# Two stacked attention blocks on one core: first transfers and keyless test reordered, context loaded in 112 and 13 rows, another merged order of the steps

## Chip, core and metric

One core of a Trainium2 chip runs the whole kernel in one launch. The metric is the device time of a launch in microseconds, as the median of the runs. The kernel before has three runs: 367.54, 370.61 and 816.39 us, median 370.61. All work is in float32, apart from masks in bf16 and a split of some operands into a high and a low part (`fp32r`).

## What is computed

A batch of 8 sequences with 112 positions of 256 features, x, and a context of 375 positions each. Cut to what matters:

```python
# block 0: 16 heads of 16 features, causal, keys and values from the context
Q, K, V = relu(x @ Wq.T + bq), relu(ctx @ Wk.T + bk), relu(ctx @ Wv.T + bv)
scores = Q K^T / 4; masked where a key's feature sum is 0, and above the diagonal
out = softmax(scores) @ V * query_mask + x
x = layer_norm(out) * gamma + beta
# block 1
q, k, v = layernorm1(x) @ wqkv;  x1 = x + softmax(causal(q k^T / 16)) v @ wproj + b
q2 = layernorm2(x1) @ wq2;  k2, v2 = layernorm2(ctx) @ wkv2
x2 = x1 + softmax(q2 k2^T / 16) v2 @ wproj2 + b2
out = x2 + relu(layernorm3(x) @ w1 + b1) @ w2 + b3
```

With the causal mask a query of block 0 sees only the first 112 context positions. A query whose visible keys are all masked gets the mean over all 375 values. Only a sequence whose first context row sums to 0 can have one, so the kernel tests the 8 first rows for that and branches around a general path (the keyless test). With these inputs the branch is not taken.

## The kernel before, in words

The batch is worked in four groups g = 0 to 3 of two sequences b = 0, 1. Each engine (TensorE = PE, VectorE = DVE, ScalarE = ACT, GpSimd = POOL, SyncE = SP) walks the same list of 322 steps, `ORDER`, and does its own share of each step; semaphores tie the shares together. `ORDER` is merged from 15 streams by the string `MIX`, where each letter takes the next step of its stream. Each stream's own order is fixed; `MIX` alone says how they interleave.

- A and E (even and odd groups): `q0 k0 v0` (projections of block 0), `xT` (transpose), `q1 k1 v1`, `t1`, `proj`, `norm2`, `xqT`, `q2`.
- C, D, I, J (even/odd group, b = 0/1), self attention: `S` (scores on PE, maxima on DVE), `M` (maxima spread to rows), `X` (scores less the maximum on PE, exponentials on ACT, causal mask on POOL), `V` (sums with the values), `O` (ACT copies the sums, PE transposes, DVE divides), `dev`, `norm`, then the same for block 1's self attention.
- P, context: `stats`, `cnorm`, then for each b `cT` (transpose), `k2`, `v2`.
- B and F (b = 0/1), cross attention: four `cS` (scores, maxima), `cM`, three `cX` (exponentials) and `cV`, `cO`, `t2`, `y` (last projection and the store).
- H (`h`, feed forward in, two for each group), K (`f`, feed forward out, one for each sequence), W (`split` of the cross weights, `shift`), N (`keys`, `masks`, `late`), R (`rows`: a bias sum on DVE), L (`flag`, `general`: the keyless test and its branch).

An engine never passes a step of its own in `ORDER`. A step that writes to PSUM claims a bank or a pair of banks, the longest filled of three pairs (`ring`), and waits until that pair's reader is done. A pair is read by DVE for `S` and `cS` (two reductions for each step) and by ACT for `X` and `cX` (two exponentials).

The keyless test: DVE sums the 8 first rows and compares (L1190, L1192), PE adds up the eight results (`flag`, L573), DVE copies the count to `any_masked` (L1206), and then PE, DVE and SP each load it into a register and branch (`general`). In `keys` DVE sums the context rows (`ksum`, L960) and makes the masks `add_mask` (L970, L971), which `S` adds first (L597).

Transfers go out from two queues. SP issues inputs, weights and results in program order, waits included; ACT issues three small ones at the start, `first_keys`, `mask_u8` and `flat_c` (vectors of biases and the identity). Lines L413 `xk_t` (transposed inputs), L419 `x_nat`, L424 `keys_nat` (tile `xh`), L429 `c_nat` (context, 125 partitions of 6 KB: two sequences of three chunks), L437 `w_qk0`, L441 `w_v0`, L452 the cross weights, L473 `w_a`, L474 `rows_sb`, L476 `w_b`. Before all steps PE runs ten matmuls on zeros, `keep_busy(10)` (L802).

Of the kernel before, what the change touches and what calls it, by code (L numbers as in the profile page):

```python
# [102 lines left out]
def b_steps(g, b):  # L103
# [14 lines left out]

MIX = ("LAALNNCANDEECDCNPICWNCWDPJEWJICPDDICPJDNDIPIAJPIAAAJCJIHHJDERPCDECEDCJDCDPAIAAKAHIJNAAAPBPBEJABPJIFFIBJICPBFEFPBEBPBBBFN"
       "DENPFBFPBEFPFEBEDCPBFBFDNKFPCDFBFBCBDCHPBDEBCKBBDCFAPBAFBFPAFDACPNBCFDCPDCPJDCBIDBBNAFAFFFJIFAAJAEIFBJFPBKFBFBIFJIPHHBPJ"  # L120
       "BIJIPEKBEEFJHIBBBIJPIBJEFIFJIJBEPFEEFBKEFEFFBBBFBFFBHBFPBFFBFFFBBBFBFKBFFFBFFBFKFF")

# [83 lines left out]
def build(nc, xk_t_d, x_nat_d, keys_d, c_nat_d, c_t_d, c_first_d, mask_d, w_d, flat_d, mask_const_d, row_d, out_d):  # L206
    ctx = ExitStack()
    with ctx:
# [195 lines left out]
        def _(sp):  # L404
# [21 lines left out]
            def load_context(g):  # L426
                if g:
                    sp.wait_ge(*a_ct.done(g - 1))
                sp.dma_start(c_nat[:, :, :, :].rearrange("p b c u -> p (b c u)"), c_nat_d[g]).then_inc(c_loaded, 16)  # L429

# [4 lines left out]
            for part in range(2):  # L435
                load_x(0, part)
                sp.dma_start(w_qk0[:, part, :, :].rearrange("p c u -> p (c u)"), w_d["qk0"][:, part * C * U:(part + 1) * C * U]).then_inc((q0_loaded, k0_loaded)[part], 16)  # L437
            sp.wait_ge(xq_loaded[0], 16)
            load_keys(0)
# [6 lines left out]
            load_x(1, 1)  # L446
            sp.wait_ge(v0_loaded, 16)
            load_context(0)
            sp.wait_ge(xk_loaded[1], 16)
            load_keys(1)  # L450
            load_queries(1)
# [44 lines left out]
        def _(pe):  # L496
# [307 lines left out]
            pe.wait_ge(prep_dve, 1)  # L804
            keep_busy(10)
            run({"shift": shifts, "flag": flag, "general": general, "f": hidden_out, "masks": masks, "q0": project_q0, "k0": project_k0, "v0": project_v0, "S": self_scores, "M": self_max_rows, "X": self_shifted,
# [7 lines left out]
        def _(act):  # L814
# [109 lines left out]

            act.dma_start(first_keys, c_first_d).then_inc(first_loaded, 16)
            act.dma_start(mask_u8[:, :], mask_d).then_inc(mask_loaded, 16)
            act.dma_start(flat_c[:, :], flat_d).then_inc(flat_loaded, 16)
# [10 lines left out]
        def _(dve):  # L938
# [12 lines left out]
            def keys(g):  # L951
                s = v_mask
                if g == 0:
                    dve.wait_ge(pads_made, 1)
                dve.wait_ge(keys_loaded[g % 2], g // 2 * 16 + 16)
                if g > 1:
                    for b in range(G):
                        dve.wait_ge(*a_exp[b].done(g - 2))
                both = slice(slot(g, 0), slot(g, G))
                s.step(nc.vector.reduce_sum(ksum[:, both], keys_nat[g % 2][:, :, :], AX.X), g, 1)  # L960
                s.step(nc.vector.tensor_copy(pad1[:, both], pad1_all[:, g * G:(g + 1) * G]), g, 2)
                after(s, g)
                s.step(nc.vector.tensor_scalar(keep0b[:, both], ksum[:, both], 0.0, None, ALU.not_equal), g, 3)
                s.step(nc.vector.tensor_scalar(pad0[:, both], ksum[:, both], 0.0, BIG, ALU.is_equal, ALU.mult), g, 4)
                s.step(nc.vector.tensor_scalar(keep1b[:, both], pad1[:, both], 0.0, None, ALU.is_equal), g, 5)
                after(s, g)
                for b in range(G):
                    if g == 0 and b == 0:
                        dve.wait_ge(mask_const_loaded, 16)
                    s.step(nc.vector.tensor_scalar(add_mask[:, 0, slot(g, b), :], causal[:, :], pad0[:, slot(g, b):slot(g, b) + 1], None, ALU.min), g, 6 + 2 * b)  # L970
                    s.step(nc.vector.tensor_scalar(add_mask[:, 1, slot(g, b), :], causal[:, :], pad1[:, slot(g, b):slot(g, b) + 1], None, ALU.min), g, 7 + 2 * b)  # L971
# [164 lines left out]
            def context_statistics(g):  # L1136
                s, n = v_ctx, G * NCH
                dve.wait_ge(c_loaded, g * 16 + 16)
                for i in range(n):
# [47 lines left out]
            for i in range(2):  # L1187
                nc.vector.memset(acc[i][:, :, :], 0.0).then_inc(prep_dve, 1)
            dve.wait_ge(first_loaded, 16)
            nc.vector.reduce_sum(first_sum[:, :], first_keys, AX.X).then_inc(flag_steps, 1)  # L1190
            dve.wait_ge(flag_steps, 1)
            nc.vector.tensor_scalar(first_masked[:, :], first_sum[:, :], 0.0, None, ALU.is_equal).then_inc(flag_steps, 1)  # L1192
            dve.wait_ge(mask_loaded, 16)
            nc.vector.tensor_scalar(pad1_all[:, :], mask_u8[:, :], BIG, None, ALU.mult).then_inc(pads_made, 1)
            dve.wait_ge(prep_act, 2)
            for e in range(2):
                nc.vector.tensor_scalar(bq0_eo[:, :, e], vec[:, VEC["bq0"]:VEC["bq0"] + C], eo_scale[:, 0, e:e + 1], None, ALU.mult).then_inc(prep_dve, 1)

# [5 lines left out]
            def general():  # L1204
                dve.wait_ge(flag_counted, 1)
                nc.vector.tensor_copy(any_masked[:, :], gen_s[:, 0:1]).then_inc(flag_made, 1)  # L1206
                dve.wait_ge(flag_made, 1)
# [102 lines left out]
```

## Time and profile before

| what | value |
|---|---|
| runs | 367.54, 370.61, 816.39 us |
| the profiled execution, its own time | 368.39 us |
| its span, first to last instruction | 366.6 us |
| outside the span | 1.8 us |
| granted TensorE clock over the span | 0.999 |
| PE busy | 346.7 us (95%) |
| DVE busy | 224.4 us (61%) |
| ACT busy | 170.6 us (47%) |
| POOL busy | 52.3 us (14%) |

All times in rows below are microseconds from the start of the span unless marked ns. A busy PE is not a PE at its peak, since a matmul record can contain time in which the next one could not yet start.

### The profile page before, as it was taken

What the parts mean: (1) busy time and instruction counts of PE and PEld (TensorE: products, weight loads), DVE (VectorE), ACT (ScalarE), POOL (GpSimd) and SP (SyncE); (2) the same over time, 40 slices, a digit from 0 to 9 for tenths busy, and PEclk for the clock granted to TensorE, in tenths of its full rate; (3) what the DMA queues carried; (4) which work ended last, traced back from release to release, by engine and by line L of the source; (5) the groups of instructions that cost most, each with busy time, mean ns of one, the idle gap of its engine ahead of it and who ended that gap; (6) DMA issues with size and microseconds to landing.
All of it is one profiled execution on the core that took longest, in us unless ns stands there. A gap on an engine that the chain in (4) does not pass through costs nothing.

```text
span 366.6 us, 9692 instructions
## 1 busy us (share of the span) xinstructions
PE 346.7 (95%) x4144; PEld 262.0 (71%) x4144; DVE 224.4 (61%) x563; ACT 170.6 (47%) x299; POOL 52.3 (14%) x67
## 2 busy tenths in 40 slices
PE   7978899999999999999999999999999999999996
PEld 4656688877965677876876786766987768675674
DVE  3879898426768746566945758556944464264412
ACT  2266652560674155674454062763453644614350
POOL 2024331040032010122100041130100031000000
PEclk9999999999999999999999999999999999999999
DMA  6759302000000002000000200000000000000000
GB/s 194 221 172 355 112 16 98 0 4 0 27 0 2 2 6 82 27 14 15 3 2 6 80 2 14 4 2 13 1 4 0 2 2 2 15 2 13 4 2 25
DMA packets 5300, 14.12 MB, mean 39 GB/s; under 512 B 689, under 2 KB 2982, under 8 KB 5002
## 3 DMA queue, kind: packets, MB, share of 16 engines
q1 hardware_dynamic: 4970, 13.42, 11.2%
q8 instruction: 33, 0.54, 0.6%
q10 hardware_dynamic: 288, 0.09, 0.1%
q14 instruction: 9, 0.07, 0.1%
HBM read 12.59 MB, written 0.92 MB: 37 GB/s over the span
## 4 chain that ended last, share of the span: by engine, by line
PE 76%; DVE 13%; DMA 5%; ACT 2%; issue 2%; SPq 1%; POOL 0%; DVEq 0%
PE ring L502 35%; PE ring L744 8%; PE acc L648 8%; PE ring L758 5%; PE ring L623 5%; DVE negmax L1032 4%; PE ring L603 3%; PE ring L597 3%; DMA xh<-in_keys 3%; PE ring L635 2%; DVE negmax L1011 2%; PE ring L667 2%; DMA w_qk<-in_w_qk 2%; PE ring L615 1%; PE ring L709 1%
## 5 line engine op out<-in xcount | busy, mean ns | idle before, releaser
L1032 DVE TENSOR_REDUCE negmax<-ring 112x2 f32<-112x750 f32 x64 | 57.0, 936 | 23.3 <-PE ring L744 22.6
L857 ACT ACTIVATE exps<-ring 125x896 f32<-125x896 f32 x48 | 41.4, 915 | 39.5 <-PE ring L758 39.2
L1247 POOL TENSOR_SCALAR_AFFINE_SELECT exps<-exps 112x896 f32<-112x896 f32 x32 | 30.9, 989 | 118.2 <-ACT exps L857 118.2
L1011 DVE TENSOR_REDUCE negmax<-ring 112x8 f32<-112x896 f32 x32 | 33.4, 1085 | 22.2 <-PE ring L603 22.1
L744 PE MATMUL ring<-k,q 32*112 32x376 f32 x256 | 38.4, 518 | 1.3 <-ACT exps L857 0.5
L648 PE MATMUL acc<-exps,v 125*17 125x112 f32 (+1 forms) x1280 | 38.7, 261 | 0.2
L648 PEld LDWEIGHTS acc<-exps,v 125*17 125x17 f32 (+1 forms) x1280 | 28.1, 97 | 12.7 <-issue 10.3
L857 ACT ACTIVATE exps<-ring,pad 112x896 f32<-112x896 f32 x32 | 30.5, 1003 | 11.3 <-PE ring L635 11.2
L502 PE MATMUL ring<-w_b,h 128*112 128x256 f32 x128 | 29.3, 382 | 0.0
L502 PEld LDWEIGHTS ring<-w_b,h 128*112 128x112 f32 x128 | 22.1, 177 | 5.8 <-issue 1.1
L502 PE MATMUL ring<-n,w_b 128*128 128x224 f32 x128 | 25.7, 357 | 0.2
L894 ACT ACTIVATE h<-ring,flat_c 128x224 f32<-128x224 f32 x32 | 11.7, 448 | 29.9 <-PE ring L502 29.9
L744 PEld LDWEIGHTS ring<-k,q 32*112 32x112 f32 x256 | 14.2, 169 | 15.2 <-issue 8.6
L502 PEld LDWEIGHTS ring<-n,w_b 128*128 128x128 f32 x128 | 23.7, 190 | 1.6 <-issue 1.4
L623 PE MATMUL ring<-maxrows,sel 32*125 32x224 f32 (+1 forms) x320 | 22.6, 318 | 1.2 <-DVE negmax L1011 0.5
L758 PE MATMUL ring<-q,k 32*125 32x224 f32 x384 | 23.1, 349 | 0.0
L623 PEld LDWEIGHTS ring<-maxrows,sel 32*125 32x125 f32 (+1 forms) x320 | 14.2, 175 | 10.7 <-issue 6.9
L502 PE MATMUL ring<-n,w_a 128*128 128x224 f32 x96 | 20.7, 362 | 0.4 <-DVE negmax L1032 0.2
L597 PE MATMUL ring<-mask_c,add_mask 112*112 112x448 bf16 x64 | 16.6, 364 | 3.5 <-DVE add_mask L971 1.1
L502 PE MATMUL ring<-wkv,ct 128*125 128x256 f32 x144 | 19.2, 287 | 0.3 <-DVE negmax L1032 0.3
L1232 POOL TENSOR_TENSOR rstd<-var_e,half 112x1 f32<-112x1 f32 x16 | 9.2, 577 | 71.6 <-DVE var_e L1124 51.5
L502 PE MATMUL ring<-ct,wkv 128*128 128x376 f32 x96 | 18.4, 341 | 0.8 <-issue 0.7
(139 smaller groups left out, 544.9 us busy)
## 6 DMA issues: line engine op xcount, KB each, us to landing
c_nat<-in_ctx SPq DMA_DIRECT2D x4, 750.0 KB
w_b<-in_w_b SPq DMA_DIRECT2D x1, 2304.0 KB, 13.3
xk_t<-in_xk_t SPq DMA_DIRECT2D x8, 224.0 KB, 4.9
w_a<-in_w_a SPq DMA_DIRECT2D x1, 1280.0 KB, 7.0
xh<-in_keys SPq DMA_DIRECT2D x4, 224.0 KB, 4.3
x_nat<-in_x SPq DMA_DIRECT2D x4, 224.0 KB, 3.2
out<-x SPq DMA_DIRECT2D x8, 112.0 KB, 1.9
rows_sb<-in_row SPq DMA_DIRECT2D x1, 560.0 KB, 8.8
```

The source lines that it names most:

```text
L502: m = nc.tensor.matmul(dst, lhs, rhs, start=start and n == 0, stop=n == len(pairs) - 1, skip_group_check=True)
L597: nc.tensor.matmul(bank(r)[0:T, 0:4 * T], add_mask[:, l, slot(g, b), :], ident_b[:, :].unsqueeze(1).to_broadcast([T, 4, T]), start=True, s ...
L603: m = nc.tensor.matmul(bank(r)[0:T, j * T:(j + 1) * T], qf[g % 2][32 * r:32 * r + 32, c, b, e, :], kf[g % 2][32 * r:32 * r + 32, c, b, :], ...
L623: nc.tensor.matmul(bank(r)[0:k, 2 * c * T:2 * (c + 1) * T], sel[rows, c:c + 1].to_broadcast([32, k]), maxrows[i][rows, :], start=c == 0, s ...
L648: m = nc.tensor.matmul(acc[s][32 * p:32 * p + VW, 2 * c + m_, 0:T], vals(8 * c + 2 * r + e), exps[0:k, EXP_AT[job], rr, j * T:(j + 1) * T] ...
L744: m = nc.tensor.matmul(bank(r)[0:T, 0:SP], q2[g % 2][rows, c, b, e, :], k2[g % 2][rows, b, c, :], start=True, stop=True)
L758: m = nc.tensor.matmul(bank(r)[0:CH, 2 * c * T:2 * (c + 1) * T], k2[g % 2][rows, b, c, ch * CH:(ch + 1) * CH], q2[g % 2][rows, c, b, :, :] ...
L857: return nc.scalar.activation(exps[0:k, EXP_AT[job], :, :], o[0:k, :, 0:4 * T], ACT.Exp, bias=bias)
L894: a_h.step(nc.scalar.activation(h[g % 2][:, 4 * i0 + i, :, :].rearrange("p b t -> p (b t)"), o[:, i // 2, (i % 2) * G * T:(i % 2 + 1) * G ...
L1011: v_max[b].step(nc.vector.tensor_reduce(negmax[0][:, slot(g, b), 2 * m_:2 * m_ + 2, :], o[0:T, :, 0:4 * T].rearrange("p r (j t) -> p r j t ...
L1032: x_max[b].step(nc.vector.tensor_reduce(negmax[1][:, b, 2 * m_:2 * m_ + 2, i], o[0:T, :, 0:S], AX.X, ALU.max, negate=True), g, 2 * i + m_ + 1)
L1247: p_masked[b].step(nc.gpsimd.affine_select(e, e, [[0, 8], [1, T]], ALU.is_ge, 0.0, base=0, channel_multiplier=-1), g, k)
```

## The change

Five edits. (1) `MIX` is another string: the same 322 steps, otherwise interleaved. (2) SP's first transfers: `mask_u8` and `first_keys` move from ACT's queue to SP's, behind the `w_qk0` pieces, and take the place of a wait for `xq_loaded`; `load_keys(1)` goes ahead of `load_context(0)` and so ahead of the wait for `xk_loaded[1]`. (3) `load_context` issues 112 rows and 13 rows as two transfers, each adding 16 to `c_loaded`. (4) `keep_busy(8)` for `keep_busy(10)`. (5) The keyless test: DVE makes `bq0_eo` before the masks and first sums; the copy to `any_masked` moves from `general` into `keys(0)`, behind the key masks and ahead of `add_mask`; and `MIX` now starts q0, k0, flag, keys(0), masks(0), general, where it started flag, q0, k0, general, keys(0), masks(0).

Of the rest of the new order: steps 6 to 13 are the old ones with the two `M` swapped. In the stretch after, sequence b = 1 of group 0 goes ahead of b = 0, where b = 0 went first; `keys(1)`, `stats(0)` and `S(1,0,0)` keep places 15, 16, 17. `rows` is step 49 (was 60), `stats(1)` 68 (was 87), `v0(3)` 173 (was 217). `keys(2)` stands right behind `xqT(0)`; `h(1,0)` and two `M` steps stood between them. The last steps on PE were

```text
y(2,1) cS(3,1,0) cX(3,0,1) cS(3,1,1) cS(3,1,2) cS(3,1,3) cV(3,0,0) cX(3,0,2) cV(3,0,1) cM(3,1) cV(3,0,2) cX(3,1,0) f(3,0)
cO(3,0) cX(3,1,1) cV(3,1,0) cX(3,1,2) t2(3,0) cV(3,1,1) cV(3,1,2) y(3,0) cO(3,1) f(3,1) t2(3,1) y(3,1)
```

and are now

```text
y(2,1) cS(3,1,0) cX(3,0,0) f(3,0) cX(3,0,1) cS(3,1,1) cS(3,1,2) cS(3,1,3) cV(3,0,0) cX(3,0,2) cV(3,0,1) cM(3,1) cV(3,0,2) cX(3,1,0) f(3,1)
cO(3,0) cX(3,1,1) cV(3,1,0) cX(3,1,2) t2(3,0) cV(3,1,1) cV(3,1,2) cO(3,1) y(3,0) t2(3,1) y(3,1)
```

```diff
-MIX = ("LAALNNCANDEECDCNPICWNCWDPJEWJICPDDICPJDNDIPIAJPIAAAJCJIHHJDERPCDECEDCJDCDPAIAAKAHIJNAAAPBPBEJABPJIFFIBJICPBFEFPBEBPBBBFN"
-       "DENPFBFPBEFPFEBEDCPBFBFDNKFPCDFBFBCBDCHPBDEBCKBBDCFAPBAFBFPAFDACPNBCFDCPDCPJDCBIDBBNAFAFFFJIFAAJAEIFBJFPBKFBFBIFJIPHHBPJ"
-       "BIJIPEKBEEFJHIBBBIJPIBJEFIFJIJBEPFEEFBKEFEFFBBBFBFFBHBFPBFFBFFFBBBFBFKBFFFBFFBFKFF")
+MIX = ("AALNNLCANDEECDCDNPIWDNDWCPJEWJIDPCCJPDICJNCPJIAPAJRAAIPCIHDJIHEPECDECPEDCJDCDIAHJIPAAJKANIAABIBJBIJPABEFCAFPBNFBEBBFPBBFC"
+       "PFBFEPNDPBEFFBDECNFDFPBBFKFPBNFBDBCFDCPHEBDEBCPBCDBFAEFAJAFCADPBBDFCPDBCNPFCIDCBDPFFAJIFAJFIFABPAKFBPAKFBIBFBJBIJPHHBIPB"
+       "JIJKEPBEEFIHJBBBIJPIBJEFIFIBJFJBPFBEFEFEPEFEFFBBFBFKFBHBFFBKBFFFBBBFBFKBFFFBFFBFFF")
...
-                sp.dma_start(c_nat[:, :, :, :].rearrange("p b c u -> p (b c u)"), c_nat_d[g]).then_inc(c_loaded, 16)
+                for rows in (slice(0, 112), slice(112, CH)):
+                    sp.dma_start(c_nat[rows, :, :, :].rearrange("p b c u -> p (b c u)"), c_nat_d[g][rows, :]).then_inc(c_loaded, 16)
...
-            sp.wait_ge(xq_loaded[0], 16)
+            sp.dma_start(mask_u8[:, :], mask_d).then_inc(mask_loaded, 16)
+            sp.dma_start(first_keys, c_first_d).then_inc(first_loaded, 16)
             load_keys(0)
...
             sp.wait_ge(v0_loaded, 16)
+            load_keys(1)
             load_context(0)
             sp.wait_ge(xk_loaded[1], 16)
-            load_keys(1)
             load_queries(1)
...
-            keep_busy(10)
+            keep_busy(8)
...
-            act.dma_start(first_keys, c_first_d).then_inc(first_loaded, 16)
-            act.dma_start(mask_u8[:, :], mask_d).then_inc(mask_loaded, 16)
             act.dma_start(flat_c[:, :], flat_d).then_inc(flat_loaded, 16)
...
+                if g == 0:
+                    dve.wait_ge(flag_counted, 1)
+                    nc.vector.tensor_copy(any_masked[:, :], gen_s[:, 0:1]).then_inc(flag_made, 1)
+                    dve.wait_ge(mask_const_loaded, 16)
                 for b in range(G):
-                    if g == 0 and b == 0:
-                        dve.wait_ge(mask_const_loaded, 16)
...
-                dve.wait_ge(c_loaded, g * 16 + 16)
+                dve.wait_ge(c_loaded, g * 32 + 32)
...
+            dve.wait_ge(prep_act, 2)
+            for e in range(2):
+                nc.vector.tensor_scalar(bq0_eo[:, :, e], vec[:, VEC["bq0"]:VEC["bq0"] + C], eo_scale[:, 0, e:e + 1], None, ALU.mult).then_inc(prep_dve, 1)
+            dve.wait_ge(mask_loaded, 16)
+            nc.vector.tensor_scalar(pad1_all[:, :], mask_u8[:, :], BIG, None, ALU.mult).then_inc(pads_made, 1)
             dve.wait_ge(first_loaded, 16)
...
             def general():
-                dve.wait_ge(flag_counted, 1)
-                nc.vector.tensor_copy(any_masked[:, :], gen_s[:, 0:1]).then_inc(flag_made, 1)
                 dve.wait_ge(flag_made, 1)
```

## Rows read from the trace of the kernel before

**Rows 1.** The page, part 1: busy time of each engine over the span.

```profile
PE 346.7 (95%) x4144; PEld 262.0 (71%) x4144; DVE 224.4 (61%) x563; ACT 170.6 (47%) x299; POOL 52.3 (14%) x67
```

**Rows 2.** Windows by stage: length, busy time, PEclk, DMA share, GB/s.

```profile
0.00:10.00 10.00, 7.35 (x28) 4.18 (x28) 4.22 (x20) 3.26 (x7) 2.08 (x7) 1.00 0.66 197
10.00:50.00 40.00, 33.59 (x444) 25.91 (x444) 34.95 (x114) 21.38 (x39) 11.75 (x13) 1.00 0.58 193
50.00:330.00 280.00, 273.59 (x3236) 209.69 (x3236) 173.35 (x412) 132.76 (x234) 38.50 (x47) 1.00 0.04 14
330.00:366.60 36.60, 32.20 (x440) 22.26 (x438) 11.91 (x20) 13.23 (x21) 0.00 (x0) 0.99 0.04 11
```

**Rows 3.** Chain of waits, first 45 us: start, length, what it waited for.

```profile
2.21 5.92 DMA w_qk<-in_w_qk
...
8.97 3.67 DMA xk_t<-in_xk_t
12.65 9.85 DMA xh<-in_keys
```

**Rows 4.** Waits of DVE, 9 to 52 us: total, times, longest.

```profile
DVE ksum L960 <- DMA xh<-in_keys: 2.5, 2, 1.6
DVE negmax L1011 <- PE ring L603: 1.4, 1, 1.4
```

**Rows 5.** Timeline of SP's issues: start, length, line, operation.

```profile
9.64 0.28 SPq L429 DMA_DIRECT2D c_nat<-in_ctx  x1
...
52.67 0.32 SPq L429 DMA_DIRECT2D c_nat<-in_ctx  x1
```

**Rows 6.** Windows around large transfers, columns as in Rows 2.

```profile
24.40:30.20 5.80, 4.71 (x98) 3.42 (x96) 5.70 (x21) 2.30 (x4) 3.11 (x3) 1.00 1.01 341
...
53.00:62.00 9.00, 9.00 (x75) 7.81 (x74) 8.02 (x22) 2.13 (x4) 1.62 (x3) 1.00 0.34 114
```

**Rows 7.** Timeline of all engines, 8 to 14 us: start, length, [idle before].

```profile
8.16 1.78 PE L502 MATMUL ring<-xk_t,w_qk 128*128 128x224 f32 x8 [1.33 <-DMA w_qk<-in_w_qk]
8.27 0.15 DVE L1206 CAST any_masked<-acc 1x1 int32<-1x1 f32 x1
...
9.33 0.69 DVE L960 TENSOR_REDUCE ksum<-xh 112x2 f32<-112x512 f32 x1 [0.92 <-DMA xh<-in_keys]
...
11.07 0.94 PE L597 MATMUL ring<-mask_c,add_mask 112*112 112x448 bf16 x4 [0.25 <-DVE add_mask L970]
...
13.02 2.09 DVE L1011 TENSOR_REDUCE negmax<-ring 112x8 f32<-112x896 f32 x2 [1.42 <-PE ring L603]
```

**Rows 8.** Timeline, POOL at 24 us: mask of the first exponentials.

```profile
24.18 1.99 POOL L1247 TENSOR_SCALAR_AFFINE_SELECT exps<-exps 112x896 f32<-112x896 f32 x2 [21.50 <-ACT exps L857]
```

**Rows 9.** Line L802, keep_busy: ns min/median/max, first and last start.

```profile
L802 PE MATMUL ring<-acc_sb x10: 379/621/634, 1.3 to 4.6; 128*128 128x512 bf16 x10
```

**Rows 10.** Groups, cS on DVE and PE: busy, mean ns, idle before.

```profile
L1032 DVE TENSOR_REDUCE negmax<-ring 112x2 f32<-112x750 f32 x64 | 57.0, 936 | 23.3 <-PE ring L744 22.6
...
L744 PE MATMUL ring<-k,q 32*112 32x376 f32 x256 | 38.4, 518 | 1.3 <-ACT exps L857 0.5
```

**Rows 11.** Timeline of DVE at 96 us: the keys of group 2.

```profile
96.30 0.69 DVE L960 TENSOR_REDUCE ksum<-xh 112x2 f32<-112x512 f32 x1 [2.42 <-DMA xh<-in_keys]
```

**Rows 12.** Timeline of PE near the end: cS, cO after cV, f.

```profile
321.71 0.90 PE L744 MATMUL ring<-k,q 32*112 32x376 f32 x8
...
324.26 0.62 PE L667 MATMUL ring<-flat_c,acc_sb 128*112 128x128 f32 x4 [0.76 <-ACT acc_sb L875]
...
358.41 3.62 PE L502 MATMUL ring<-w_b,h 128*112 128x256 f32 x16
```

**Rows 13.** Chain of waits, 334 to 340 us.

```profile
334.79 0.95 DVE negmax L1032
...
336.97 0.93 ACT exps L857
...
338.87 0.95 DVE negmax L1032
```

More of the change, by code:

```diff
@@ L117 @@
            "R": [("rows",)], "L": [("flag",), ("general",)]}
-MIX = ("LAALNNCANDEECDCNPICWNCWDPJEWJICPDDICPJDNDIPIAJPIAAAJCJIHHJDERPCDECEDCJDCDPAIAAKAHIJNAAAPBPBEJABPJIFFIBJICPBFEFPBEBPBBBFN"
-       "DENPFBFPBEFPFEBEDCPBFBFDNKFPCDFBFBCBDCHPBDEBCKBBDCFAPBAFBFPAFDACPNBCFDCPDCPJDCBIDBBNAFAFFFJIFAAJAEIFBJFPBKFBFBIFJIPHHBPJ"
-       "BIJIPEKBEEFJHIBBBIJPIBJEFIFJIJBEPFEEFBKEFEFFBBBFBFFBHBFPBFFBFFFBBBFBFKBFFFBFFBFKFF")
+MIX = ("AALNNLCANDEEDCDNPIWDNDWCPJEWJIDPCCJPDICJNCPJIAPAJRAAIPCIHDJIHEPECDECPEDCJDCDIAHJIPAAJKANIAABIBJBIJPABEFCAFPBNFBEBBFPBBFC"
+       "PFBFEPNDPBEFFBDECNFDFPBBFKFPBNFBDBCFDCPHEBDEBCPBCDBFAEFAJAFCADPBBDFCPDBCNPFCIDCBDPFFAJIFAJFIFABPAKFBPAKFBIBFBJBIJPHHBIPB"
+       "JIJKEPBEEFIHJBBBIJPIBJEFIFIBJFJBPFBEFEFEPEFEFFBBFBFKFBHBFFBKBFFFBBBFBFKBFFFBFFFBFF")
 def merged():
@@ L1192, in _ @@
             nc.vector.tensor_scalar(first_masked[:, :], first_sum[:, :], 0.0, None, ALU.is_equal).then_inc(flag_steps, 1)
[L1193 to L1197, printed above, removed]
             def rows_summed():
```

## Prediction

> **What bounds the kernel now.** I read the page's engine line first, then windows by stage, then for each stage the chain of waits or the waits of the engine that the windows point at. Over the whole span PE is busy 346.7 of 366.6 us and nothing else is near that [rows 1]. So no reordering can win much: what it can win is PE's idle time, 19.9 us, and the waits that hide inside PE's busy records. The windows say where the idle time lies [rows 2]: 2.65 us before 10 us, 6.41 us from 10 to 50, 6.41 us in the 280 us of the middle, 4.4 us in the last 36.6. The reader is to see that the stage from 10 to 50 us is another kernel than the rest: DVE works 34.95 of 40 us there, and DVE, not PE, is the one that runs without a break. In the middle PE is at 98% and DVE at 62%.
>
> In that second stage DVE's waits have names [rows 4]: 1.4 us for the first scores, and 2.5 us in two waits for the context rows `xh` (L960), the longest 1.6. By subtraction the other is 0.9, the one at 9.33 us [rows 7]; so the 1.6 us belongs to the keys of group 1. The chain of waits shows why they are late [rows 3]: SP stands 3.67 us until `xk_t` of group 1 is in, issues the keys only at 12.65, and they need 9.85 us to land, at 22.5. What they queue behind is `c_nat`, issued at 9.64 [rows 5].
>
> **Context in two transfers.** The `c_nat` issued at 52.67 [rows 5] shows what that load is: 9 us at a DMA share of 0.34 and 114 GB/s, together 1.03 MB, which is the context and one load of queries (0.23 MB), while large weight transfers reach a share of 1.01 and 341 GB/s [rows 6]. So 125 partitions keep about a third of the 16 DMA engines busy and the keys behind them share those. The Trainium skill (DMA: Bandwidth & Descriptors, section on why a DMA increments its semaphore by 16) says that the number of engines is the largest up to 16 that divides the slowest dimension: 5 for 125, 16 for 112, 13 for 13. The trace's 0.34 agrees with 5 of 16. By my rows: 768 KB (750 KiB) at the 192 to 245 GB/s class of this stage (197 before 10 us, 193 after [rows 2]) is 3.9 us in place of about 9. Cost: one more issue on SP, 0.3 us [rows 5], four times, with nothing queued behind it on SP that is urgent. For groups 1 to 3 the gain is nil: no DVE wait on `c_nat` stands among the waits [rows 4], and the steps between `cT` and the next `stats` cover even 9 us. If that cover were gone in one group it would cost at most the present 9 us less the new 4, and the change makes that less likely, not more. In group 0 the split is what keeps `c_nat` from delaying `stats(0)`, queries and cross weights; it is worth its part of the next term.
>
> **Keys of group 1 ahead of the context.** They are issued at about 9.7 in place of 12.65, behind three loads of 224 KB that are in at 12.6 (8.97 + 3.67 [rows 3]); one more of that size at 197 GB/s takes 1.2 us, so they land at about 14, seven us before DVE asks (22.5 - 1.6 = 20.9). What is next late? The context follows to about 18, queries of group 1 (229 KB) to 19, cross weights (524 KB) to 22; their users come at 22.7 (`stats(0)`) and 23.2 or later (`split`). So DVE's 1.6 us go entirely: DVE does `keys(1)`, `stats(0)` and the maxima of `S(1,0,0)` 1.6 us earlier. PE does not collect it at once, since the first `V` waits for POOL's mask at 24.18 + 1.99 [rows 8], which hangs on ACT and not on the keys; but the stage is DVE's, and from its chain the gain reaches PE when PE becomes the bound at 50 us. **Term: -1.6 us**, bounds 0 (all swallowed by the POOL and ACT chain) and -2.5 (all of DVE's DMA waits).
>
> **Keyless test and first transfers.** Two things move against each other. DVE now enters `keys(0)` without the register load and branch that it made between 8.42 (end of L1206) and 9.33 [rows 7]; the key sums can start when the keys land. But `flag` on PE is now behind `k0`, whose weights land at 8.13 (2.21 + 5.92 [rows 3]) and which ends at 8.16 + 1.78 = 9.94. Two tiny matmuls and their signal take some 0.2 us, the copy 0.15, so the count is there at 10.3, and `add_mask` behind it at 10.4, about as now. Then PE has to load the count and branch before `S(0,0,0)`: the same operation took DVE at most 0.91 (8.42 to 9.33), so PE reaches S at 10.3 + 0.9 = 11.2, against 11.07 now [rows 7]. DVE's own branch falls into its 1.42 us wait for these scores, so it is covered; without that cover it would cost 0.9. SP keeps the place of its keys: two issues of 0.43 replace a wait that ended at the same time. `mask_u8` and `first_keys` land later (about 8), with 0.7 us of DVE work behind them, just before `keys(0)` starts; who waits behind them is `keys(0)`, which waits for its rows anyway. `flat_c` is issued a us earlier; its users run ahead of `k0`'s weights and win nothing. **Term: +0.2 us**, bounds -0.4 and +0.7.
>
> **keep_busy(8).** The two matmuls removed stood ahead of `q0`, and after `q0` PE waits 1.33 us for `k0`'s weights [rows 7]: hidden, 0. The ten of L802 take from 634 down to 379 ns, median 621 [rows 9]: most at the lower level (1.2 GHz), a few at 2.4 GHz. I take these to be the last ones, so the clock rises within the ten, and the 1.33 us of idle time after `q0` did not lower it, since `k0` took its 1.78 us at PEclk 1.00. The Trainium skill (TensorE: Matmul & The Clock Gate, Part 1) says that the clock rises only after PE has been busy for a while and falls after idleness; a shorter warm-up speaks against this edit. It is a rival below.
>
> **The last steps.** `f(3,0)`, 3.6 us [rows 12], now stands ahead of the run of four `cS`, and no `f` stands behind `cO(3,1)`. Gain: that run is bound by the readers of its banks; 0.95, 0.93 and 0.95 us of the chain there are DVE and ACT, not PE [rows 13]. With 3.6 us of other PE work in between, the first DVE piece goes for sure, the ACT piece perhaps, the last not, because three `cS` still follow each other: -0.95 to -1.9. Loss: `cO(3,1)` now stands right behind `cV(3,1,2)` and waits for ACT's copy, which the same pair cost 0.76 at 324.26 [rows 12]; `y(3,0)` still covers DVE's division behind it. Net between -1.1 and +0.8 (if the run of `cS` gains nothing); I take **-0.3**.
>
> **The middle order.** PE's visible idle time is 6.41 us, but `cS` hides more: 38.4 us over 32 steps is 1.20 us each [rows 10], where one that did not wait took 0.90 [rows 12]: 9.6 us. DVE needs 2 x 0.936 = 1.87 us for each, twice what PE needs, so each `cS` wants about 1 us of other PE work beside it. I counted in both orders the `S` and `cS` steps that directly follow another one: 7 before, 6 now. Elsewhere distances change both ways: `h` to its `f` and `q1` to `S` get tighter in one group each, `cO` to `t2` too, `X` to `V` looser. `keys(2)` right behind `xqT(0)` makes DVE wait up to 3.5 us in place of 2.42 [rows 11], with an `X` and two projections of 1.78 us each [rows 7] as cover. The context going in faster changes nothing here. **Term: -0.5 us**, bounds -4 and +5: half of the hidden waits either way.
>
> **Sum.** Against the profiled execution, 368.4 us (span 366.6 and 1.8 around it): -1.6 + 0.2 + 0 - 0.3 - 0.5 = -2.2, so **366.2 us**. The median of the runs before, 370.6, lies 2.2 above that execution and the fastest run 0.9 below it, and I forecast on the scale of the profiled one; a median that lies as high again would be 368.4.
>
> **Rivals.**
> *The gain is swallowed.* The 1.6 us are lost to POOL and ACT, whose first mask [rows 8] does not move, or to a new late load. For it: PE's `V` waits there. Against it: DVE, not PE, is busy without break. 366.2 + 1.6 = 367.8.
> *Slower: the cS of the new middle wait longer.* Place: `cS` behind `cS` or `S`, PE waiting for DVE's reductions. Price: half as much again as the 9.6 us hidden now, +4.8, hence 366.2 + 4.8 = 371.0. It decides from 2.2 us on, that is from a mean of 1.27 us for each `cS`. Against it: one fewer direct pair, and the same average load.
> *Faster: the new middle clears half of these waits.* 366.2 - 4.8 = 361.4.
> *The clock stays low.* With eight matmuls the rise comes only in or after `k0`. `k0` at half the rate adds 1.78 us on the path, 368.0, more if it lasts. Against: some of the ten are fast, and `q0` follows closely on the eighth.
>
> **How the numbers follow.** Chances: forecast 0.60 (own range 364.5 to 368.4), swallowed 0.14, slower middle 0.12, faster middle 0.11, clock 0.03. The range leaves out half of the two middle rivals' cases and takes in the higher median: 362.8 to 370.2. Two per cent, about what a measurement of this kernel can tell from no change, is 7.4 us of 370.6. Faster by more than that needs under 363.2: most of the faster middle, 0.09. Slower by more needs over 378: 0.02. Within: 0.89.
>
> **What the profile after should show.** SP issues the keys of group 1 before 10 us and they land before 15; DVE's wait for `xh` at 22.5 is gone, `stats(0)` starts near 22.7 and PE's idle time from 10 to 50 falls by 1 to 2 us. After `c_nat` of group 1 the DMA share is near 1 for some 3 us. `S(0,0,0)` starts at 11.0 to 11.5. PE stands about 0.8 us before `cO(3,1)`. Mean `cS` between 1.1 and 1.25 us. The prediction is wrong if `cS` leaves that band, if another transfer than the keys holds DVE before 30 us, or if the first matmuls after `q0` run at the lower clock.

## The result and the profile after

Six runs of the kernel after lie between 363.47 and 364.18 us, median **364.1**. Six of the kernel before, three of them new, have a median of 367.35. The ratio, which leaves out the run of 816.39 us, is 0.9903, interval 0.9877 to 0.9929: 1% faster, 3.3 us, inside the forecast's range and 2.1 us under its 366.2, and within the two per cent that it named as the likely class. The profiled execution took 364.14 us (span 362.4, which is 4.2 less than before, where the forecast had 2.2). The two numbers differ because the profiled execution of the kernel before, 368.39 us, lies 1.0 above the median of its runs, and that of the kernel after does not: some 0.9 of the 4.2 belongs to that one execution. In code lines of after, most lines of before are two higher: L744 is L746, L1011 is L1013.

The page's engine line and the windows by stage answer to [rows 1] and [rows 2].

```profile
PE 345.5 (95%) x4142; PEld 263.0 (73%) x4142; DVE 228.0 (63%) x563; ACT 170.9 (47%) x299; POOL 52.7 (15%) x67
```

```profile
0.00:10.00 10.00, 8.11 (x28) 5.22 (x28) 5.37 (x28) 3.95 (x9) 2.08 (x7) 1.00 0.76 185
10.00:50.00 40.00, 35.23 (x480) 26.86 (x480) 35.95 (x109) 21.95 (x40) 11.69 (x13) 1.00 0.59 195
50.00:330.00 280.00, 274.68 (x3244) 212.28 (x3244) 177.96 (x413) 132.84 (x235) 38.97 (x47) 1.00 0.05 15
330.00:362.40 32.40, 27.50 (x398) 18.67 (x392) 8.74 (x16) 12.19 (x17) 0.00 (x0) 0.99 0.03 9
```

PE's idle time fell from 19.9 to 16.9 us: 0.8 before 10 us, 1.6 from 10 to 50, 1.1 in the middle, while the end has 0.5 more. The other 1.2 us left PE's busy records, in which waits hide.

The start: the chain of waits of after (first group), its timeline (second), SP's issues (third) and DVE's waits from 9 to 52 us (fourth), beside [rows 3 to 5] and [rows 7].

```profile
1.26 3.60 PE ring L804 x8
4.86 2.66 PE ring L504 x8
7.63 1.82 ACT qf L829 x4
...
20.44 0.59 DVE ksum L960
...
22.21 1.98 DVE c_stats L1142 x6
```

```profile
4.65 4.37 PE L504 MATMUL ring<-xk_t,w_qk 128*128 128x224 f32 x16
...
10.46 0.94 PE L599 MATMUL ring<-mask_c,add_mask 112*112 112x448 bf16 x4 [0.98 <-ACT kf L822]
```

```profile
8.68 0.33 SPq L424 DMA_DIRECT2D xh<-in_keys  x1
9.05 0.88 SPq L430 DMA_DIRECT2D c_nat<-in_ctx  x2
```

```profile
DVE negmax L1013 <- PE ring L605: 2.0, 1, 2.0
DVE sd L1081 <- POOL sd_r L1232: 0.2, 1, 0.2
```

No DMA stands among DVE's waits from 9 to 52 us any more. The wait for `k0`'s weights, 1.33 us [rows 7], is gone as well: `q0` and `k0` are now one run of 16 matmuls, and what `S(0,0,0)` waits for is ACT's copy of `kf`. It starts at 10.46, 0.6 earlier than before, where I had 0.1 later.

The groups of `cS`, beside [rows 10]:

```profile
L1034 DVE TENSOR_REDUCE negmax<-ring 112x2 f32<-112x750 f32 x64 | 56.9, 935 | 19.3 <-PE ring L746 18.8
...
L746 PE MATMUL ring<-k,q 32*112 32x376 f32 x256 | 37.8, 518 | 1.3 <-DVE negmax L1034 0.5 <-ACT exps L859 0.4 <-ACT qf L829 0.3
```

1.18 us for each `cS` where it was 1.20. The end on PE, beside [rows 12], and the chain there, beside [rows 13]:

```profile
356.10 0.62 PE L669 MATMUL ring<-flat_c,acc_sb 128*112 128x128 f32 x4 [0.76 <-ACT acc_sb L877]
```

```profile
328.14 0.95 DVE negmax L1034
...
335.22 0.93 ACT exps L859
...
337.13 0.95 DVE negmax L1034
```

The forecast 0.76 is there, and all three pieces of DVE and ACT are still in the chain.

**Where the 4.2 us come from.** To compare two orders I took the start of each projection in a trace and subtracted the PE work of all steps ahead of it, at one fixed price for a step (0.9 us for a `cS`, 3.0 for an `h`, and so on from their undisturbed records). What is left is time that PE lost up to there; the mean over 24 us of work, less that of before, is the lead. It is good to some 0.4 us; a column mixes what happens within 12 us of work on either side of it. All of it is one execution against one, and that of before is 1.0 above its median. The last column is the difference of the spans.

```text
PE work done before (us)   10    50    110   170   230   290   span
after                      1.1   2.0   3.5   2.6   4.9   4.9   4.2
old order, edits 2 to 5    0.6   0.4   0.4   0.3   0.3   0.3   0.3
new order alone           -1.6  -1.3   0.2  -0.7   1.6   1.6   0.9
only keys(1) moved         0.3   0.8   0.8   0.8   0.8   0.9   0.8
after, keys(1) back        1.5   2.4   3.8   2.9   5.2   5.3   4.5
after, one context load    2.0   2.8   4.3   3.4   5.7   5.7   4.6
after, both of these       1.1   1.5   3.0   2.1   4.4   4.4   3.3
new to step 133, then old  1.7   2.6   4.1   3.9   3.9   3.9   3.9
old to step 133, then new  1.5   2.0   2.0  -2.1   0.2   0.3  -0.5
```

The first two columns can be read without a price, since up to `v1(0)` both orders often have the same kinds of step behind them. There the kernel after is ahead by 0.6 us at each step from `S(0,0,0)` to `k0(1)`, and by 1.6 at each of `v0(1)`, `k2(0,0)`, `q1(0)` and `v1(0)`. At `q0(1)` and at `v1(0)` the lead is 1.0 and 2.0 for "old to step 133, then new", 1.1 and 1.1 for "after, both of these", and -0.2 and 0.8 for "only keys(1) moved". So the start gives 0.6, the stage to 50 us 1.0, the middle 3.3, and the last stretch takes 0.7 back.

The start is also where executions differ most. `S(0,0,0)` starts between 9.44 and 10.74 in the eleven kernels that have edit (5), and at 11.07 and 11.23 in the two with the old first steps.

### The profile page after: what moved, and what is told of

It reads as the page before. It is cut to its first block, busy times and chain, and to the rows that moved or that the text cites. A ratio compares the mean times of both kernels' runs of the same rounds, so it can differ in the third digit from the quotient of the medians.

```text
span 362.4 us, 9692 instructions
## 1 busy us (share of the span) xinstructions
PE 345.5 (95%) x4142; PEld 263.0 (73%) x4142; DVE 228.0 (63%) x563; ACT 170.9 (47%) x299; POOL 52.7 (15%) x67
## 4 chain that ended last, share of the span: by engine, by line
PE 82%; DVE 11%; ACT 4%; issue 2%; ACTq 0%
PE ring L504 39%; PE ring L746 8%; PE acc L650 7%; PE ring L625 5%; PE ring L760 5%; PE ring L605 4%; DVE negmax L1034 4%; PE ring L599 3%; PE ring L637 3%; DVE negmax L1013 2%; PE ring L669 2%; ACT exps L859 2%; PE ring L711 1%; PE ring L536 1%; PE ring L617 1%
## 5 line engine op out<-in xcount | busy, mean ns | idle before, releaser
L1013 DVE TENSOR_REDUCE negmax<-ring 112x8 f32<-112x896 f32 x32 | 33.4, 1085 | 22.1 <-PE ring L605 22.0
L746 PE MATMUL ring<-k,q 32*112 32x376 f32 x256 | 37.8, 518 | 1.3 <-DVE negmax L1034 0.5
L746 PEld LDWEIGHTS ring<-k,q 32*112 32x112 f32 x256 | 14.1, 169 | 13.7 <-issue 8.6
L504 PEld LDWEIGHTS ring<-n,w_a 128*128 128x128 f32 x96 | 17.5, 190 | 2.7 <-issue 2.1
## 6 DMA issues: line engine op xcount, KB each, us to landing
w_b<-in_w_b SPq DMA_DIRECT2D x1, 2304.0 KB, 12.4
```

What stands on the lines that cost most here:

```text
L504: m = nc.tensor.matmul(dst, lhs, rhs, start=start and n == 0, stop=n == len(pairs) - 1, skip_group_check=True)
L746: m = nc.tensor.matmul(bank(r)[0:T, 0:SP], q2[g % 2][rows, c, b, e, :], k2[g % 2][rows, b, c, :], start=True, stop=True)
L1013: v_max[b].step(nc.vector.tensor_reduce(negmax[0][:, slot(g, b), 2 * m_:2 * m_ + 2, :], o[0:T, :, 0:4 * T].rearrange("p r (j t) -> p r j t ...
```

## The experiments

Each was timed beside the kernel before, whose median was 367.43, 367.42 and 367.38 us in the three groups of runs.

**Edits 2 to 5 without the new order.**

```diff
-MIX = ("AALNNLCANDEEDCDNPIWDNDWCPJEWJID...
+MIX = ("AALNNLCANDEECDCNPICWNCWDPJEWJIC...   (old order from step 7 to the end)
```

> All edits of the change except the order behind the first six steps: MIX is AALNNL and then the old string. If the start and the middle gain separately, as the two traces suggest (lead of the changed kernel 1.6 to 2.2 us at 50 us, about 5 at 326, then 1 lost), this kernel keeps the start's part: 1.5 to 2.2 us faster than before, ratio 0.994 to 0.996, with scores S(0,0,0) reduced at about 12.4 and keys(1) at about 20.3. Rival, the new order collects everything and the start's gain is swallowed by PE later: ratio 0.998 to 1.000. Rival, the start alone gives all: 0.990.

366.94 us, ratio 0.9989 (0.9966 to 1.0013), span 366.3. The profile is of an execution 1.1 above the median. `xk_t` of group 1 and so SP's own branch (16.72) came late in it, DVE stood 1.4 us for them, and PE behind it:

```profile
19.54 1.75 PE L504 MATMUL ring<-xk_t,w_qk 128*128 128x224 f32 x8 [1.86 <-DVE negmax L1013]
```

That took its lead down to 0.3. The last kernel below has the same first 133 steps and the same other edits, did not have this wait, and is 2.0 ahead from `v0(1)` to step 133. By the medians these edits are worth 0.5 us by themselves, by the ratio 0.4, and neither is clear of zero.

**The new order without edits 2 to 5.**

```diff
-MIX = ("LAALNNCANDEECDCNPIC...
+MIX = ("AALNNLCANDEEDCDNPIW...   (all else as before)
```

> The kernel before with only the new MIX, no transfer, split, keep_busy or keyless edit. If the middle order gains 2 to 3 us by itself, ratio 0.991 to 0.995, with the DVE wait for the keys of group 1 (until about 22.5 us) still there. If the new order pays only together with the earlier keys and context, ratio 0.997 to 1.002.

367.32 us, ratio 0.9978 (0.9957 to 1.0), span 365.7. By the medians that is 0.1 us, by the ratio 0.8. So neither part alone gives as much as 1 us, and together they give 3.3. The timeline of PE and the windows of this kernel show why:

```profile
12.12 0.93 PE L597 MATMUL ring<-mask_c,add_mask 112*112 112x448 bf16 x4 [1.92 <-issue]
12.99 1.41 PE L603 MATMUL ring<-kf,qf 32*112 32x112 f32 x32
14.32 3.26 PE L502 MATMUL ring<-w_v,xk_t 128*112 128x256 f32 x8
```

```profile
10.00:20.00 10.00, 8.08 (x86) 6.01 (x87) 5.33 (x20) 1.24 (x3) 0.00 (x0) 0.83 0.71 200
```

With the old place of the copy to `any_masked` DVE makes it only behind `masks(0)`, at 10.90, and PE stands 1.92 us before its branch. Behind that the granted clock is 0.83 over ten microseconds: L603 takes 1.41 us and `v0` 3.26, where in the kernel after they take 1.05 and 1.98. That is 1.6 us behind the kernel before at the start. From 50 us of work to the end the new order gains 2.2 us, as much as in the kernel after. Nine of its twelve runs had a mean clock of 0.993 to 0.995 and took 366.96 to 367.64 us; the three at 0.998 or more took 365.46 to 366.13. So the fall of the clock is in most executions and costs some 1.7 us, and at the full clock the new order alone is 1.3 to 2.0 us faster than before.

**Only the keys of group 1 moved.**

```diff
             sp.wait_ge(v0_loaded, 16)
+            load_keys(1)
             load_context(0)
             sp.wait_ge(xk_loaded[1], 16)
-            load_keys(1)
```

> The kernel before with one edit: the keys of group 1 issued ahead of the context. My step says DVE's wait of 1.6 us at 22.5 goes and stats(0) does not wait in its place, since the unsplit context then lands at about 22 and is asked for at 22.7: span 1.2 to 1.6 us shorter, ratio 0.995 to 0.997. Rival: the context on a third of the engines, and the queries and cross weights behind it, become late instead and DVE or ACT wait for them: ratio 0.998 to 1.001.

367.19 us, ratio 0.9995 (0.9968 to 1.0022), span 365.8. DVE's waits from 9 to 52 us:

```profile
DVE negmax L1011 <- PE ring L603: 1.4, 1, 1.4
DVE ksum L960 <- DMA xh<-in_keys: 0.9, 1, 0.9
```

The 1.6 us of DVE are gone, of 2.5 only 0.9 is left, and `stats(0)` starts 1.6 us earlier (22.75). PE at the masks of `S(1,0,0)`, first the kernel before, then this one:

```profile
24.14 0.96 PE L597 MATMUL ring<-mask_c,add_mask 112*112 112x448 bf16 x4 [1.15 <-DVE add_mask L971]
```

```profile
23.08 0.59 PE L597 MATMUL ring<-mask_c,add_mask 112*112 112x448 bf16 x2
24.25 0.59 PE L597 MATMUL ring<-mask_c,add_mask 112*112 112x448 bf16 x2 [0.59 <-ACT exps L857]
```

PE starts them 1.06 us earlier, but then stands 0.59 for ACT's exponentials, which did not move. DVE gets to the maxima of these scores 0.83 earlier (26.20 for 27.03), and PE is 0.83 ahead from `S(1,0,1)` on, where it was 0.16 behind up to `X(0,0,0)`. So against this profile 1.0 of the 1.6 us reaches PE, and 0.6 is swallowed as the rival has it.

The runs give less: 0.2 us. The likely reason is the execution that was profiled before. In it 15 of the 16 increments of the semaphore for these keys were there at 20.28 and the last at 22.50, and DVE asked at 20.91. The kernel with the new order alone has the same transfers, and there the last came at 20.87. So most of the 1.6 us seems to be one late increment in one execution; a second profile of the kernel before would show it, and there is none.

**Keys back, context back, and both.** The kernel after with `load_keys(1)` behind the context and the wait again, with the context in one transfer, and with both.

```diff
-            load_keys(1)
             load_context(0)
             sp.wait_ge(xk_loaded[1], 16)
+            load_keys(1)
```

```diff
-                for rows in (slice(0, 112), slice(112, CH)):
-                    sp.dma_start(c_nat[rows, :, :, :]...
+                sp.dma_start(c_nat[:, :, :, :]...
```

> The changed kernel with the context ahead of the keys of group 1 again, but still split in 112 and 13 rows. By my step the keys then land behind a context that takes 3 to 4 us: at about 17.5, still ahead of DVE at 20.3, and nothing is lost; ratio as the changed kernel's 0.990. So the split and the swap would be two cures for one delay. Rival: SP's wait for xk_loaded[1] holds the keys long enough that DVE waits 1 us or more at 20.3.

> The kernel after with each context load in one transfer of 125 rows again, keys of group 1 still ahead of it. Theory (the keys are what counts, either edit alone gets them in early enough): the keys land at 14 to 15 us as before this edit, stats(0) starts up to 1.5 us later because the context lands at about 20 to 21.6 instead of 17.4, queries and weights behind it follow; time 364.1 (span 362.4), up to 0.5 more. Rival (the split is worth something of its own in group 0, because stats(0) and the cross weights now stand on the chain of DVE): 364.8 to 365.5. Context of groups 1 to 3 lands about 9 us after its issue instead of 4, and no engine waits for it.

> The kernel after with the context in one transfer and the keys of group 1 behind it, that is with neither of the two edits. With only the keys moved back (run before this one) the keys still landed at 16.7 and the time stayed at 363.98. Theory (the two edits give the same thing, so that one may go but not both): keys land at about 20.5 to 22.5, DVE waits for them again (about 1.5 to 2.5 us, since it now reaches them earlier), and the time is 0.8 to 1.6 above the kernel after: 364.9 to 365.7. Rival (the whole stage is bound by POOL's mask and ACT's exponentials, the keys never counted): 364.1 to 364.4 although DVE waits.

363.98 us (ratio 0.990), 364.3 (0.9905) and 364.88 (0.9916). The keys are issued at 12.86 with the first edit undone and yet are in at 16.7, as nothing slow lies ahead of them: the two context transfers are in at 15 to 16 us. With the context in one transfer DVE waits 0.7 us for it, at 21.9, and no more. Only with both undone does DVE wait for the keys, for 0.55 us and for SP's issues before:

```profile
DVE negmax L1012 <- PE ring L604: 2.0, 1, 2.0
DVE x_nat L1001 <- SPq L472: 1.0, 1, 1.0
DVE ksum L959 <- DMA xh<-in_keys: 0.5, 1, 0.5
```

PE's lead does not grow from `q0(1)` to `v1(0)` then (1.1 at both, with 0.2 between them behind DVE's wait for SP), where it grows by 0.8 to 1.0 in the other two and in the kernel after. The median is 0.8 higher, the ratio 0.0013 (0.5 us), which is inside the intervals of about 1 us to either side. So moving the keys and splitting the context, edits (2) and (3), do the same thing, either suffices in these runs, and together they are worth 0.5 to 0.8 us, not clear of noise.

**The small transfers back on ACT's queue.** Edit (2) without the keys.

```diff
-            sp.dma_start(mask_u8[:, :], mask_d).then_inc(mask_loaded, 16)
-            sp.dma_start(first_keys, c_first_d).then_inc(first_loaded, 16)
+            sp.wait_ge(xq_loaded[0], 16)
...
+            act.dma_start(first_keys, c_first_d).then_inc(first_loaded, 16)
+            act.dma_start(mask_u8[:, :], mask_d).then_inc(mask_loaded, 16)
             act.dma_start(flat_c[:, :], flat_d).then_inc(flat_loaded, 16)
```

> The changed kernel with mask_u8 and first_keys back on ACT's queue ahead of flat_c, and the wait for xq_loaded back. If these small transfers on the second queue are what made one DMA engine late, the weights of k0 land at 8.0 to 8.3 us again in place of 6.4 to 6.8, and S(0,0,0) is reduced from about 13.0 in place of 12.0 to 12.4: span 0.5 to 0.8 us longer than the changed kernel's. Rival: the lateness of that engine was chance, and k0 starts by 6.9.

365.0 us, ratio 0.993 (0.9901 to 0.9959), 1.0 above the kernel timed beside it that has only the keys back. `flat_c` is in at 6.3 in place of 3.6, and DVE's `bq0_eo`, the masks and the test behind it start late. The scores are reduced at 12.69, where they are at 11.4 to 12.4 in the ten kernels with the edit. But the profile does not show that `flat_c` is the cause: `k0` ends at 9.29 here and 9.02 in the kernel after, and `S(0,0,0)` starts 1.45 and 1.44 us behind that. So what costs the 1.0 us stays open. `k0`'s weights are in at 6.87, as in the other kernels with the new DVE part (5.87 to 6.89 in all eleven), while they need 7.96 to 8.28 in the three kernels with the old one. So the early weights don't come from emptying ACT's queue.

**Ten matmuls of keep_busy in the kernel after.**

```diff
-            keep_busy(8)
+            keep_busy(10)
```

> The kernel after with ten matmuls on zeros instead of eight. In the kernel after all eight ran at the lower clock level (608 to 634 ns) and q0's first matmuls too, so that q0 took 2.66 us instead of about 1.8. Theory: the rise of the clock depends on how long PE has worked, not on what it works on, so two more matmuls push q0 back by 1.0 to 1.25 us, q0 then runs at the full level (1.8 us), and k0 starts 0.2 to 0.4 us later than now unless its weights are late: time 364.1 to 364.4, no difference. Rival (the prediction's zero holds only because k0's weights were late; now that they land at 6.8 they are not): 0.3 to 0.6 slower, 364.4 to 364.7.

364.29 us, ratio 0.9907 (0.9872 to 0.9942), span 362.4 as with eight. Timeline of PE:

```profile
1.26 4.45 PE L804 MATMUL ring<-acc_sb 128*128 128x512 bf16 x10 [1.26 <-DVE ones L1181]
5.50 3.45 PE L504 MATMUL ring<-xk_t,w_qk 128*128 128x224 f32 x16
```

`q0` and `k0` take 3.45 us behind ten and 4.37 behind eight, and end at 8.95 and 9.02. That looks as if the clock gave back what the two matmuls cost, but the two executions differ in more than that. One matmul of `q0` takes 581 ns before the clock rises and 352 after (the windows by stage have a granted clock of 1.00 in both parts, so it is the durations that tell), and the rise stands at 6.98 us in the kernel after and at 6.03 here. Over all kernels, with eight or ten, it lies between 4.2 and 7.2. Where it came at 6.02 with eight matmuls (neither of the two load edits), `k0` ends at 8.52 and `S(0,0,0)` starts at 9.97, 0.44 earlier than here (10.41). So at a like rise the edit is worth some 0.4 us at the start, and in the medians 0.2, which is within the noise.

**The last steps.** Both have the new order to step 296. The first keeps the new place of `cX(3,0,0)`, behind `cS(3,1,0)`, and moves the two `f` and `y(3,0)` back; the second is the old order from step 297 on, with `cX(3,0,0)` ahead of `y(2,1)`.

```diff
-...FKBHBFFBKBFFFBBBFBFKBFFFBFFFBFF")
+...FKBHBFFBBFFFBBBFBFKBFFFBFFBFKFF")      (first)
+...FKBHBBFFBFFFBBBFBFKBFFFBFFBFKFF")      (second)
```

> The changed kernel with the last 25 steps in the old order: f(3,0) behind cX(3,1,0) and f(3,1) behind cO(3,1), cX(3,0,0) stays where the change has it. By the traces the new tail loses: from y(2,1) to the end 36.2 us with one cX more (1.2) against 33.9, a loss of 1.1 us. So 0.5 to 1.3 us faster than the changed kernel, about 5 us faster than before, ratio 0.986 to 0.989. My prediction's step said the new tail gains 0.3; then this kernel is 0.3 us slower than the changed one, ratio 0.991.

> The changed kernel with the old order for all of the last 26 steps, so cX(3,0,0) ahead of y(2,1) too. From y(2,1) to y(3,1) PE took 30.07 us in the kernel before, 32.34 in the changed one with a cX of 1.2 us more, and 32.07 with only the two f moved back. If the remaining loss lies in cX(3,0,0) standing behind cS(3,1,0), that stretch comes out at about 30.1 here and the span about 1.1 us below the changed kernel, near 361.3. Rival: the banks that the new middle leaves behind make the difference, and the span is that of the changed kernel within 0.3.

363.92 us (ratio 0.9919, 0.989 to 0.9949, span 361.8) and 365.07 (0.9932, 0.99 to 0.9964). The `f` steps ahead of the run of `cS` gain nothing: with them or without them the chain has 0.95 of DVE, 0.93 of ACT and 0.95 of DVE there. By the medians (363.92 and 364.1) moving them is a loss of 0.2 us, by the ratios (0.9919 and 0.9903) a gain of 0.6, so nothing is shown. With `cX(3,0,0)` ahead of `y(2,1)` the kernel is 0.5 us (ratios) to 1.1 (medians) slower. Its profile, of an execution of 370.01 us, shows where:

```profile
327.56 0.48 PE L625 MATMUL ring<-maxrows,sel 32*125 32x224 f32 x8 [1.64 <-ACT maxrows L855]
```

```profile
330.00:346.40 16.40, 15.69 (x145) 9.38 (x144) 7.98 (x11) 3.67 (x5) 0.00 (x0) 0.50 0.03 8
```

The new middle leaves `cM(3,0)` directly ahead of this `cX`. In the old order `t2(2,1)` and `v2(3,1)` stood between them, and in the kernel after `y(2,1)` and `cS(3,1,0)` do. ACT still has four outputs of `h` (1.46 us) to do before the maxima that `cX` needs, and PE stands 1.64 us at the full clock. Behind that the granted clock was 0.50 for 17 us. Seven of its twelve runs had a clock of 0.998 or more and took 364.48 to 365.09, and four others at 0.989 to 0.994 took 366.37 to 368.11. So the move of `cX(3,0,0)` is no gain over the old end; it covers a wait that the new middle would otherwise make.

**New order to step 133 and the old behind it, and the mirror of it.**

```diff
-       "PFBFEPNDPBEFFBDECNFDFPBBFKFPBNF...
+       "PFBFEPNDPBEFFPEBEDPBFBFDNKFPCDF...   (first: remaining steps in the old order)
...
-MIX = ("AALNNLCANDEEDCDNPIW...
+MIX = ("AALNNLCANDEECDCNPIC...             (second: to step 133 the old, then the new)
```

> The changed kernel with the new order for the first 133 steps alone and the old one after (M(2,0,0) done early, stats(2) first). PE's lead over the kernel before was 2.0 us at 50 us of work, 3.3 at 130 and 4.9 from 240 on. If each stretch keeps its own gain, this kernel holds about 3.3 us at 130 and loses nothing later: span 363.3 with the old tail (366.6 - 3.3). Rival: the gain of the second stretch only existed as an echo of the first, then 361.5 or so here too; or the first does not last without the second, then 365 or more.

> The kernel after with the old order for steps 7 to 133 (the first six as after, which the test needs) and the new order for all that is left. The mirror of it, new to step 133 and old behind, took 364.99 (span 362.7). The stretches of that one: it had all of its gain by step 133 and none behind. Theory A (the stretches add up): all but 0.9 of the gain goes, 365.7 to 366.3. Theory B (they replace each other: an order behind step 133 that has more other work between the cS catches up on part of what the old one left waiting): 364.6 to 365.4. If 366.7 or more, the new order of the last 189 steps is worth nothing by itself.

364.99 us (ratio 0.9928, 0.9891 to 0.9965, span 362.7) and 369.5 us (1.0036, 1.0001 to 1.0071, span 367.1). Both my theories failed for the second: it is slower than before. The table shows three things. In the first kernel the new order gains 1.7 us between `v1(0)` and step 133 over the old, and the old one does not give it back: from there on each step is 3.9 us ahead of before. From 170 on it gains 2.3 us in the second kernel too, as it does in the kernel after. But in between the second loses 4.1 us, at the seam. Timeline of its PE, and windows:

```profile
148.15 0.94 PE L760 MATMUL ring<-q,k 32*125 32x224 f32 x16
151.15 0.40 PE L617 MATMUL ring<-ident_r,spread 112*128 112x112 f32 x2 [2.06 <-DVE spread L1019]
...
151.98 2.51 PE L504 MATMUL ring<-n,w_a 128*128 128x224 f32 x8
```

```profile
145.00:150.00 5.00, 4.09 (x74) 3.32 (x72) 3.80 (x13) 2.71 (x6) 0.00 (x0) 1.00 0.15 49
150.00:155.00 5.00, 3.85 (x26) 3.11 (x30) 3.15 (x20) 2.26 (x6) 1.33 (x1) 0.78 0.00 0
155.00:165.00 10.00, 10.00 (x138) 7.21 (x135) 2.80 (x5) 4.93 (x7) 3.85 (x4) 0.94 0.04 13
```

At the seam `stats(2)` stands two steps ahead of `M(2,0,0)`, and DVE does it first:

```profile
147.63 2.04 DVE L1142 BATCH_NORM_STATS2 c_stats<-c_nat 125x6 f32<-125x256 f32 x6
```

Only then, at 150.60, does DVE begin `spread`, which `M` needs. PE stands 2.06 us, and behind that it works at a granted clock of 0.78. One of its six runs had the clock at 0.999 over the span in place of 0.995, and that one took 367.4 where the others took 368.9 to 369.8. So a badly set wait of 2 us cost another 1.5 to 2.4.

## Why the prediction was right, and where it was not

Direction and class were right, and the time lies in the range given (362.8 to 370.2), but 0.4 us below the own range of the likeliest case (364.5 to 368.4). The bound (PE's idle time of 19.9 us, and no reordering can win much) held. Point by point, in spans:

- **Keys of group 1, -1.6: mis-sized, measured -1.0 between the profiles and -0.2 in the runs.** Every sign came as described: issued at 8.68, in at 14.4, DVE's wait gone, `stats(0)` at 22.2 in place of 24.3. Two steps failed. "From its chain the gain reaches PE when PE becomes the bound": PE waits for ACT's exponentials as well, and 0.6 of the 1.6 us was swallowed there, as the rival said. And the 1.6 us was read as the kernel's own wait from one execution that lies 1.0 above the median, in which one increment of the keys came 2.2 us behind the others. That the runs show only 0.2 fits this, without proving it. The new order adds nothing from 10 to 50 us: with the load edits PE's lead grows by 1.0 there in the old order (the last kernel) as in the new, and with both of them undone not at all.
- **Context in two transfers, "worth its part of the next term": right, as far as the runs can tell.** Each of the two load edits can go alone; without both the median is 0.8 us higher. Group 1's context is issued at 51.3 and in at 56.3, 5 us where it was 9.4 (52.7 to 62.1), and no engine collects that; the nil for groups 1 to 3 holds.
- **Keyless test and first transfers, +0.2 (-0.4 to +0.7): wrong in sign, measured -0.6 at `S(0,0,0)`.** I took the landing of `k0`'s weights at 8.13 over unchanged; it was 6.78. With `k0` ended 0.92 us earlier (9.02 for 9.94) the load and branch of PE also lie beside ACT's copy, so that my 0.9 us for them isn't on the path. The value of the edit is seen in the new order without it: it prevents 1.92 us of waiting and what the clock adds, and 0.98 us of waiting for `kf` is left.
- **keep_busy(8), 0: right within the noise, not for the reason given.** The wait that I named as the cover is gone, and at a like rise of the clock the start is 0.4 us earlier with eight. The rival's sign did not come: `k0` runs at 352 ns a matmul, the full level. But `q0` was partly at the lower one, 2.66 us in the chain. That the clock rises within the ten, as I took it, holds for the profile before (4.2 us) and not for ten matmuls in general (6.0 and 6.7 us in two other kernels with ten).
- **The last steps, -0.3 (-1.1 to +0.8): the predicted gain of 0.95 did not come, the loss of 0.76 did.** The stretch took 0.7 in all; for the part that I had priced the runs give +0.2 by medians and -0.6 by ratios. Three `cS` in a row go on waiting whatever stands ahead of the first. The moved `cX(3,0,0)` was in the list and got no price; it covers a wait of 1.64 us that the new middle makes.
- **The middle order, -0.5 (-4 to +5): mis-sized, measured -3.3 before the last stretch.** Between the forecast and the faster rival (-4.8 below the forecast). But it isn't the mechanism that I or the rival named: mean `cS` went from 1.20 to 1.18 us, 0.6 us in all. That the bounds held it is luck as far as the mechanism goes. The new order wins in two stretches, 1.9 us from `v1(0)` to 110 us of PE work and 2.3 between 170 and 230, and gives 0.9 back between. PE's idle time fell ahead of some groups (before the masks of `S`, L597, from 3.5 to 2.7 us, before `y` from 1.1 to 0.5, before the transposes of `xh` from 0.7 to 0.1) and rose ahead of others (before `h` from 0.2 to 0.9, before `cT` from 0 to 0.7). I did not isolate single pairs of steps, so which moves do it stays open; that it is the order is shown, and so is, with one profile each, that the first stretch gives its gain with the old order behind it, and the second with the old order ahead of it or without edits 2 to 5.

Against the forecast, in spans, the keys came out 0.6 us worse and the end 1.0 worse, the start 0.8 better and the new order 2.8 better: 2.0 in sum, the difference of -4.2 and -2.2. The sum was nearer than its terms, and that is luck: errors of both signs met. In the runs the gain is 3.3, and the 0.9 between fits a keys term near 0.2.

## What to carry to other kernels

An order written out by hand and the edits that serve it are one thing: here either half alone gave less than 1 us and both 3.3, in good part because the new order without its earlier test makes PE stand 1.9 us and mostly lose its clock too. Look first for the single waits near 2 us that an order makes, since here three of four cost about double or more, through the clock. When two edits relieve the same queue, price them together and try each without the other. Before a wait in a trace is priced, ask whether that execution is a usual one: the profile that I worked from was 1.0 us above the median, and its largest single term, a DMA wait of 1.6 us, gave 1.0 against that profile and 0.2 in the runs. A gain on the second busiest engine reaches the bound only after the waits for the third are counted.

## What the chip showed that I had not expected

- After 1.92 and 2.06 us without a matmul the granted clock fell to the lower level (1.2 GHz) for a few microseconds: 0.83 over 10 to 20 us, 0.78 over 150 to 155 us. After 1.64 us it was at 0.50 for 17 us. But after 1.86 us (edits 2 to 5 alone, 17.7 to 19.5 us) it stayed at 1.00. The same `v0` took 3.26 and 1.98 us. Waits of up to 1.37 us did not do that in any of the profiles. So a wait of this length can cost the clock and need not; what decides it is open.
- In the fourteen profiles the first rise of the clock, as the durations of the matmuls show it, stands anywhere from 4.2 to 7.2 us, with eight matmuls of `keep_busy` (4.5 to 7.2) as with ten (4.2 to 6.7). It is part of why the start of the scores differs by up to 1.3 us between kernels that begin alike.
- The semaphore of the context transfer was raised in 5 steps as its data landed before and in 29 after, which fits five DMA engines for 125 partitions, and sixteen and thirteen for 112 and 13. The same bytes took 5 us instead of 9.4.
- `k0`'s weights, issued at the same 2.2 us, landed between 5.87 and 6.89 in eleven kernels and between 7.96 and 8.28 in three. What sets that is open.
